# Moving the second attention's weight products and constants, regrouping the first attention's softmax by half, and storing the query squares without padding

## The chip, the cores and the metric

One Trainium2 chip, one of its cores. The metric is the device time of one execution in microseconds, taken as the median of several runs. A profile of one more execution stands beside them; all times inside the kernel come from that one.

## The reference: what is computed

A small vision tower in float32 on 16 images of 3 x 96 x 96. Its parts, in the order of the computation:

```python
h = tok(x)                                  # 36 patches of 16x16x3, layer norm, @ lin_w, layer norm, + class token and positions
h = h + attn0(layernorm(h))                 # 16 query heads of 16, one shared key and value head, rows batch x (head, token)
h = h + moe(layernorm(h))                   # 8 experts of 128, two chosen per token, and a shared one of 256
h = h + attn1(layernorm(h))                 # 16 heads of 16, attention over the HEADS' rows, three rounds
h = h + ffn(layernorm(h))                   # 256 -> 768 -> 256, weights and activations rounded to grids
```

There are 37 tokens per image, 592 in all, of width 256. The second attention is the one whose weights the change moves:

```python
for it in range(3):
    ql = qcur @ Wlq.T + blq;  kl = kcur @ Wlk.T + blk;  vl = vcur @ Wlv.T + blv     # 16 x 16, every head the same
    qs = ln(ql, lnc_w) * tscale;  ks = ln(kl, lnd_w)
    ai = softmax(qs @ ks.T / 4) @ vl
    qcur = qcur + ai;  kcur, vcur = kl, vl
```

In the kernel only the first 16 tokens of each image take part in the second attention as queries and keys (the reference slices them), so one round has 2 halves of 8 images with 256 columns each.

## The kernel before

The stages around the change, with their places:

- **Token embedding and first layer norms.** TensorE: patches x `lin_w` in three banks `y` 0, 1, 2 (L1635). VectorE: for each `y`, bias, statistics, norm, addend (L1048 to L1071); it asks ScalarE for the inverse root in between (`variance_given`, L958; `root_of_tiles`, L646). Then `layer_norm(2)` (L985) writes `xn`, tile by tile (L994). Behind `y` TensorE turns four weights (`wT` q0, o0, v1, o1) and `wkvT` (L1645), has 8 fillers, and forms the small matrices of the second attention (`wl`, `wn`, `bl`, `bq`, L1659 to L1672), which VectorE masks by head after its layer norm (L1074 to L1082). Then `turn(0)` with 10 fillers (L1696) transposes `xn`.
- **First attention.** Keys and query groups (L1710 to L1718), values (`v0`, L1719), logits of half 0 and of half 1 (`S`, L1728; 16 partitions, 37 columns each). VectorE subtracts the row maximum (`scores`, L1115), ScalarE takes exponentials (`exps`, L704), VectorE sums and inverts (`row_sums`, L1122), GpSimd multiplies (L569). VectorE interleaves halves: scores 0,0 0,1 0,2, sum 0,0, scores 0,3, then a sum of half 0 with a score of half 1 in turn. ScalarE's list alternates exponentials of half 1 with emptying of the banks below.
- **Weights of the second attention.** Behind both halves of logits TensorE computes powers of the small matrices (`pw` 0, 1), four composed weights (`wc` q, 1, 2, 3) and the constants (`cst`), L1788 to L1816. Then probabilities of half 0 are transposed (`PT`, L1750), multiplied with the values (`PV`, L1767), and so on; the projection (`wo`) follows.
- **Second layer norm.** `turn(1)` with 22 fillers (L1842), gate logits `lg` (L1846), the experts (L1866). VectorE rounds the feed-forward weights `fraw` between its expert steps (`dequantise`, L1168), after one wait for their DMAs ahead of the loop (L1253).
- **Third layer norm.** TensorE turns six banks of rounded weights (`fw`), then `turn(2)` with 6 fillers (L1882).
- **Second attention, three rounds.** Per round: logits of half 0, `query_variance` (L1925), logits of half 1, and so on. ScalarE squares the queries into `squares_n` (L812), which has the padded layout of `queries_n` (two blocks of 16 columns apart by 16), zeroed once by GpSimd (L573). TensorE then needs two products per group of 128 rows, one for each half f of the width.

DMAs that hang on these places: SyncE issues the experts' weights when `y` 2 is full (L479) and the feed-forward weights when `cst` is full (L488).

The main lines:

```python
for u in range(2):                                        # L1785
    attention_scores(u)
...
for n, name, m in (("q", "q1", q_), (1, "k1", KEY_POWER[0]), (2, "k1", KEY_POWER[1]), (3, "k1", KEY_POWER[2])):   # L1797
...
turn(1, 2, awake=22)                                      # L1842
...
ins = product(b[:, u * B + n * NH:u * B + (n + 1) * NH],  # L1932
              [(squares_n[:, u, at_ + 32 * CB * f + TF * (1 - f):...], mean_m[:, :, 0]) for f in range(KD)])
```

## Time and profile before

| what | us |
|---|---|
| median of 3 runs | 312.52 |
| lowest and highest | 310.95 and 314.73 |
| the profiled execution | 311.37 |
| its span, first to last instruction | 309.6 |
| TensorE busy | 258.7 |
| VectorE busy | 207.3 |
| ScalarE busy | 95.6 |
| GpSimd busy | 43.0 |

Times inside the kernel count from the first instruction of the span. The profiled execution is 1.77 us longer than its span, which is what lies around it. The mean granted clock of TensorE over the span is 0.956 of full speed. In the profile PE is TensorE, PEld its loading of stationary operands, DVE VectorE, ACT ScalarE, POOL GpSimd, SP SyncE. A row such as `PE bank L1608` names the engine, the tile written and the line; L1608 is the helper `product`, so the operands in the row tell which product it is.

### The profile page before, as it was taken

The page shows a single profiled execution, that of the slowest core. Times are in us where ns is not written, and L with a number is a line of the kernel's source. Part 1 is how long each engine was busy: PE and PEld are TensorE (multiplying, and loading weights), DVE is VectorE, ACT ScalarE, POOL GpSimd, SP SyncE. Part 2 cuts the span into 40 slices and gives each one's busy share as a digit, 9 for nine tenths or more (in the row PEclk, how much of TensorE's full clock was granted, in tenths as well). Part 3 has the DMA queues.
Part 4 walks back from the last instruction along what each step waited for, and adds up shares of the span by engine and source line. Part 5 has one row for each costly group of instructions (what it writes and reads, how often), then busy time and mean ns, then how long its engine had stood idle before and what let it go on. Part 6 is the DMA issues. An engine that isn't in the chain of part 4 may idle for free.

```text
span 309.6 us, 5714 instructions
## 1 busy us (share of the span) xinstructions
PE 258.7 (84%) x2276; PEld 212.8 (69%) x2276; DVE 207.3 (67%) x495; ACT 95.6 (31%) x226; POOL 43.0 (14%) x77
## 2 busy tenths in 40 slices
PE   1068999799989999999999989997769599907596
PEld 1047889698987867777776878784658376607484
DVE  0679388538705459788878946858587545999931
ACT  0045033223551251111112244744504232953000
POOL 6032001012600200000000016694000000000000
PEclk9999999995799999999999999999999899987689
DMA  7933009600062000000000000000000000000001
GB/s 180 314 62 70 2 14 300 197 4 2 2 226 83 3 0 0 0 2 0 0 2 1 0 2 0 4 2 2 1 2 0 2 0 0 0 0 3 0 34 44
DMA packets 16148, 12.10 MB, mean 39 GB/s; under 512 B 4603, under 2 KB 15578, under 8 KB 16122
## 3 DMA queue, kind: packets, MB, share of 16 engines
q1 hardware_dynamic: 13864, 10.01, 11.7%
q10 hardware_dynamic: 2258, 1.73, 1.8%
q8 instruction: 18, 0.29, 0.4%
q14 instruction: 8, 0.07, 0.1%
HBM read 11.13 MB, written 0.61 MB: 38 GB/s over the span
## 4 chain that ended last, share of the span: by engine, by line
PE 63%; DVE 18%; SPq 7%; ACT 6%; issue 4%; DMA 1%; DVEq 0%; ACTq 0%
PE bank L1608 46%; PE bank L2058 5%; SPq L465 3%; PE bank L1603 3%; PE bank L1705 3%; DVE part L1456 2%; PE bank L1767 2%; DMA cols<-in_L_attn_factor 1%; DVE big L1040 1%; ACT big L916 1%; ACT big L917 1%; DVE big L1522 1%; PE bank L1684 1%; ACT xT L686 1%; SPq L467 1%
## 5 line engine op out<-in xcount | busy, mean ns | idle before, releaser
L1608 PE MATMUL bank<-xT,big 128*128 128x296 f32 (+1 forms) x192 | 45.7, 391 | 0.0
L1608 PEld LDWEIGHTS bank<-xT,big 128*128 128x128 f32 x192 | 34.3, 190 | 9.5 <-issue 0.2
L1603 PE MATMUL bank<-ident,ones 128*128 128x128 f32 x172 | 26.0, 317 | 6.4 <-POOL queries_n L542 6.4
L1603 PEld LDWEIGHTS bank<-ident,ones 128*128 128x128 f32 x172 | 24.8, 229 | 7.3 <-POOL queries_n L542 6.4
L1608 PE MATMUL bank<-xT,fT 128*128 128x296 f32 (+12 forms) x96 | 26.2, 437 | 2.4 <-DVE xT L1477 2.4
L1608 PEld LDWEIGHTS bank<-xT,fT 128*128 128x128 f32 x96 | 18.1, 201 | 9.5 <-issue 2.7
L1608 PE MATMUL bank<-big,cur 128*128 128x256 f32 (+1 forms) x100 | 23.3, 381 | 0.7 <-DVE cur L1230 0.7
L779 ACT ACTIVATE cen<-bank 128x296 f32<-128x296 f32 x20 | 8.3, 417 | 46.4 <-PE bank L1608 40.7
L1608 PEld LDWEIGHTS bank<-big,cur 128*128 128x128 f32 (+1 forms) x100 | 18.0, 182 | 4.9 <-DVE cur L1230 1.5
L1243 DVE SCALAR_TENSOR_TENSOR h<-bank,route,h 128x256 f32<-128x256 f32 (+1 forms) x40 | 17.0, 477 | 2.9 <-PE bank L1608 2.9
L1456 DVE TENSOR_REDUCE part<-big 128x1 f32<-128x296 f32 (+2 forms) x18 | 13.1, 732 | 8.1 <-ACT big L909 8.0
L588 POOL TENSOR_SCALAR big<-keys_n,k_w 128x256 f32<-128x256 f32 x24 | 15.9, 683 | 4.6 <-DVE keys_n L1335 4.6
L2058 PE MATMUL bank<-fT,big 128*128 128x256 f32 (+1 forms) x60 | 15.4, 424 | 0.5 <-DVE big L1453 0.5
L1608 PE MATMUL bank<-big 128*128 128x256 f32 (+1 forms) x60 | 13.2, 380 | 1.9 <-DVE big L1040 1.9
L2058 PEld LDWEIGHTS bank<-fT,big 128*128 128x128 f32 (+1 forms) x60 | 12.4, 208 | 3.4 <-DVE big L1453 0.8
L1608 PEld LDWEIGHTS bank<-big 128*128 128x128 f32 (+1 forms) x60 | 10.8, 182 | 4.0 <-issue 2.1
L1608 PE MATMUL bank<-probs,rsd 37*128 37x257 f32 (+1 forms) x10 | 4.6, 648 | 10.1 <-DVE first L977 10.1
L1011 DVE BATCH_NORM_STATS2 st<-big 96x6 f32<-96x256 f32 x18 | 6.1, 408 | 10.1 <-DMA big<-in_x 10.1
L1230 DVE TENSOR_TENSOR cur<-cen,bank 128x296 f32<-128x296 f32 x20 | 9.0, 460 | 4.8 <-PE bank L1608 4.4
L580 POOL COPY cur<-xT 128x256 f32<-128x256 f32 x2 | 0.8, 408 | 77.5 <-ACT xT L688 77.5
L2026 PE MATMUL bank<-ident,mx 128*128 128x128 f32 x4 | 1.3, 333 | 11.8 <-DVE mx L1459 10.0
L1608 PEld LDWEIGHTS bank<-probs,rsd 37*128 37x128 f32 (+1 forms) x10 | 3.0, 312 | 11.2 <-DVE first L977 10.4
(294 smaller groups left out, 496.7 us busy)
## 6 DMA issues: line engine op xcount, KB each, us to landing
big<-in_x SPq DMA_DIRECT2D x3, 576.0 KB, 10.6
big<-in_L_ffn_w_gate SPq DMA_DIRECT2D x2, 512.0 KB, 5.4
big<-in_L_ffn_w_up SPq DMA_DIRECT2D x2, 512.0 KB, 6.5
big<-in_L_ffn_w_down SPq DMA_DIRECT2D x1, 1024.0 KB, 8.7
big<-in_L_tok_lin_w SPq DMA_DIRECT2D x3, 256.0 KB, 9.9
small<-in_L_ffn_w_gate SPq DMA_DIRECT2D x1, 768.0 KB, 4.6
small<-in_L_ffn_w_up SPq DMA_DIRECT2D x1, 768.0 KB, 6.5
small<-in_L_ffn_w_down SPq DMA_DIRECT2D x1, 768.0 KB, 9.2
```

The costliest lines, as they stand in the source:

```text
L465: sp.dma_start(col[:, 2 * c:2 * c + 2], v[c], allow_slow_non_contiguous=True).then_inc(cols_in, 16)
L588: ins = pool.tensor_scalar(fkeys[a - 1][:, u, :, n, :], keys, k_w[:, a - 1, n:n + 1], 1.0, ALU.mult, ALU.mult)
L779: empty(act.activation(silu[:, c, :], b[:, 0:HP], ACT.Silu))
L1011: ins = dve.bn_stats(st[0:96, 3 * w + c, :], pv[:, c, :, w, :])
L1230: empty(dve.tensor_tensor(hid[:, e % 3, c * HP:(c + 1) * HP], silu[:, c, :], b[:, 0:HP], ALU.mult))
L1243: ins = dve.scalar_tensor_tensor(out=v, in0=src, scalar=route[0:n, t, e:e + 1], in1=v, op0=ALU.mult, op1=ALU.add)
L1456: return dve.tensor_reduce(part[:, n:n + 1], v, AX.X, ALU.max, apply_absolute_value=True)
L1603: pe.matmul(b[:, 0:P], ones[:, :], ident[:, :], start=True, stop=True)
L1608: ins = pe.matmul(out_, a_, b_, start=(n == 0), stop=(n == len(pairs) - 1))
L1705: ins = pe.matmul(b[32 * j:32 * j + m, at_:at_ + 4 * T].rearrange("p (u c) -> p u c", u=2), w(k), xq[:, k, :, 2 * j * T:2 * (j + 1) * T], ...
L1767: ins = pe.matmul(b[32 * q:32 * q + 32, m * 2 * T:(m + 1) * 2 * T].rearrange("p (i t) -> p i t", i=2), vals[0:G3, 3 * u + g, s, h_, :], by ...
L2058: ins = pe.matmul(b[0:rows, 0:D], gate[:, o * NT + t * P:o * NT + t * P + rows], fT[2][:, o, :], start=(o == 0), stop=(o == FC - 1))
```

## The change

1. TensorE and VectorE form and mask the small matrices (`wl`, `wn`, `bl`, `bq`) between `y` 1 and `y` 2; VectorE does so while it waits for the root of `y` 1.
2. `pw` 0, `pw` 1, `wc` q and `wc` 1 move ahead of `turn(0)`; the transposes of v1 and o1, `wc` 2 and `wc` 3 move between the first attention's projection and `turn(1)`; the constants `cst` move between `fw` and `turn(2)`. ScalarE's emptying moves with them. Fillers go from 8 to 0 (`wl`), 10 to 2, 22 to 0 and 6 to 0.
3. The values' product and its handling by VectorE and GpSimd stand between the two halves of the logits; VectorE and ScalarE do all of half 0, then all of half 1.
4. The squares of the queries are stored densely, in order image, f, token; one product per group of 128 rows. GpSimd's zeroing and ScalarE's wait for it go.
5. The feed-forward weights' DMAs wait for `wc` 3; VectorE waits for them at its first reduction. The experts' weights still wait for `y` 2, which comes later. The query bias constant is computed early, with its own semaphore.

The diff, cut to its core:

```diff
 def fills():
-    for i in range(3):
+    for i in range(2):
         f.append((("y", i), "dve"))
-    for n in ("q0", "o0", "v1", "o1"):
-        f.append((("wT", n), "act"))
-    f.append((("wkvT",), "act"))
     f.append((("wl",), "dve"))
     f.append((("wn",), "dve"))
     f.append((("bl",), "dve"))
     f.append((("bq",), "act"))
+    f.append((("y", 2), "dve"))
+    f.extend((("wT", n), "act") for n in ("q0", "o0"))
+    f.append((("wkvT",), "act"))
+    f.extend((("pw", n), "act") for n in range(2))
+    f.extend((("wc", n), "act") for n in ("q", 1))
...
-    f.append((("v0",), "dve"))
     for u in range(2):
         f.extend((("S", u, j), "dve") for j in range(4))
-    f.extend((("pw", n), "act") for n in range(2))
-    f.extend((("wc", n), "act") for n in ("q", 1, 2, 3))
-    f.append((("cst",), "act"))
+        if not u:
+            f.append((("v0",), "dve"))
...
+    f.extend((("wT", n), "act") for n in ("v1", "o1"))
+    f.extend((("wc", n), "act") for n in (2, 3))
...
     f.extend((("fw", n), "dve" if n % 2 else "act") for n in range(6))
+    f.append((("cst",), "act"))
...
-            filled(sp, ("cst",))
+            filled(sp, ("wc", 3))
...
             for u in range(2):
+                if u:
+                    values_by_slot()
                 for j in range(4):
                     pool.wait_ge(sums_ready, 4 * u + j + 1)
...
-            pool.memset(squares_n[:, :, :], 0.0).then_inc(squares_cleared, 1)
...
             for j in range(2):
                 root_of_tiles(j)
+            b = take(act, ("bq",))
+            empty(act.copy(bqh[:, :], b[:, 0:2 * NH]))
+            attn_weight("q0")
+            attn_weight("o0")
             b = take(act, ("wkvT",))
             empty(act.copy(wkvT.rearrange("p k n d -> p (k n d)"), b[:, 0:4 * HD]))
             root_of_tiles(2)
+            for n in range(2):
+                powers(n)
...
             inverse_root(P, slice(0, TT))
+            for n in ("q", 1):
+                composed_weights(n)
             turned(0)
...
             for j in range(4):
                 exps(0, j)
-            powers(0)
-            exps(1, 0)
...
+            for j in range(4):
+                exps(1, j)
             for t in range(RT):
                 probs_turned(0, t)
...
+            attn_weight("v1")
+            attn_weight("o1")
+            composed_weights(2)
             inverse_root(P, slice(0, TT))
+            composed_weights(3)
             turned(1)
...
+            constants()
             turned(2, c_lna, (0, 2))
...
-                act.activation(padded(squares_n, u), padded(queries_n, u), ACT.Square).then_inc(q_squared, 1)
+                act.activation(squares_n[:, u, :].rearrange("p (b f t) -> p f b t", b=CB, f=KD),
+                               queries_n[:, u, TF:].rearrange("p (f b t) -> p f b t", f=KD, t=2 * TF)[:, :, :, 0:TF],
+                               ACT.Square).then_inc(q_squared, 1)
...
-                variance_given(ins)
+                variance_given(ins, small_matrices if j == 1 else None)
...
-            scores(0, 0)
-            scores(0, 1)
-            scores(0, 2)
-            row_sums(0, 0)
-            scores(0, 3)
...
+            for j in range(4):
+                scores(0, j)
+            values()
+            for j in range(4):
+                row_sums(0, j)
+            for j in range(4):
                 scores(1, j)
-            row_sums(1, 0)
-            scores(1, 3)
-            for j in range(1, 4):
+            for j in range(4):
                 row_sums(1, j)
...
                 if step == 0:
+                    dve.wait_ge(ffn_in, 48)
...
             for j in range(3):
                 b = fill(("y", j))
...
+                if j == 1:
+                    pe.wait_ge(attn_w_in, 16 * N_ATTN_W)
+                    small_matrices()
...
+            attn_weight("q0")
+            attn_weight("o0")
...
+            emptied(pe, ("bl",))
+            for n in range(2):
+                if n:
+                    emptied(pe, ("pw", 0))
+                b = fill(("pw", n))
...
+            composed_weights("q", "q1", q_)
+            composed_weights(1, "k1", KEY_POWER[0])
...
-            turn(0, 1, awake=10)
+            turn(0, 1, awake=2)
...
-            for u in range(2):
-                attention_scores(u)
...
+            attention_scores(0)
+            values_of_tokens()
+            attention_scores(1)
...
-            turn(1, 2, awake=22)
+            attn_weight("v1")
+            attn_weight("o1")
+            composed_weights(2, "k1", KEY_POWER[1])
+            emptied(pe, ("pw", 1))
+            composed_weights(3, "k1", KEY_POWER[2])
+            turn(1, 2)
...
-            turn(2, 3, awake=6)
+            pe.wait_ge(q_bias_ready, 1)
...
+            turn(2, 3)
...
                     for n in range(2):
-                        at_ = 32 * 4 * n
                         ins = product(b[:, u * B + n * NH:u * B + (n + 1) * NH],
-                                      [(squares_n[:, u, at_ + 32 * CB * f + TF * (1 - f):at_ + 32 * CB * f + TF * (1 - f) + P],
-                                        mean_m[:, :, 0]) for f in range(KD)])
+                                      [(squares_n[:, u, n * P:(n + 1) * P], mean_m[:, :, 0])])
```

## Rows read from the trace of the kernel before

**Rows 1.** The page: busy time by engine, and granted clock in 40 slices.
```profile
PE 258.7 (84%) x2276; PEld 212.8 (69%) x2276; DVE 207.3 (67%) x495; ACT 95.6 (31%) x226; POOL 43.0 (14%) x77
...
PEclk9999999995799999999999999999999899987689
```
**Rows 2.** Windows: length, busy time of each engine (instructions), then granted clock, DMA share, GB/s.
```profile
70.90:81.00 10.10, 9.53 (x88) 9.16 (x87) 9.71 (x24) 5.09 (x10) 3.29 (x5) 0.50 0.00 0
...
248.00:249.00 1.00, 1.00 (x5) 0.73 (x4) 0.22 (x1) 0.41 (x1) 0.00 (x0) 0.86 0.00 0
```
**Rows 3.** The chain that ended last, in order of time: start, length, what.
```profile
44.55 1.75 PE bank L1649 x16
...
67.95 2.40 PE bank L1736 x80
...
76.20 10.05 PE bank L1608 x68
...
87.00 1.78 ACT cur L712 x5
...
89.02 2.27 PE bank L1767 x123
...
100.73 4.91 PE bank L1603 x44
...
244.40 15.65 PE bank L1608 x52
```
**Rows 4.** TensorE's timeline: start, busy, line, instruction, count, idle before.
```profile
77.64 5.35 PE L1608 MATMUL bank<-wlT,small 128*128 128x128 f32 x32
...
175.90 1.50 PE L1603 MATMUL bank<-ident,ones 128*128 128x128 f32 x12
177.77 1.79 PE L1684 MATMUL bank<-ident,xn 128*128 128x128 f32 x10 [0.36 <-DVE xn L994]
...
189.97 1.95 PE L1608 MATMUL bank<-mean_m,qT 128*128 128x8 f32 x16
```
**Rows 5.** GpSimd's timeline: softmax factors, and keys spread over heads.
```profile
82.61 2.34 POOL L569 TENSOR_TENSOR big<-big,row_sum 128x370 f32<-128x370 f32 x3 [0.86 <-DVE row_sum L1126]
...
185.73 4.89 POOL L588 TENSOR_SCALAR big<-keys_n,k_w 128x256 f32<-128x256 f32 x4 [4.59 <-DVE keys_n L1335]
...
199.98 6.08 POOL L588 TENSOR_SCALAR big<-keys_n,k_w 128x256 f32<-128x256 f32 x10
```
**Rows 6.** VectorE's timeline: layer norms, small matrices, softmax of the first attention.
```profile
43.76 0.25 DVE L1060 BATCH_NORM_AGGREGATE mv<-st 128x2 f32<-128x6 f32 x2
44.61 0.16 DVE L1064 TENSOR_TENSOR masked<-rstd,passes 128x2 f32<-128x2 f32 x1 [0.60 <-ACT rstd L644]
...
47.70 0.40 DVE L1053 TENSOR_TENSOR h<-bank,sqr 80x256 f32<-80x256 f32 x1
...
54.05 0.68 DVE L1075 TENSOR_TENSOR wlT<-bank,head_of 128x512 f32<-128x512 f32 x1
...
54.91 0.16 DVE L1085 TENSOR_SCALAR temps<-temps 128x3 f32<-128x3 f32 x1
...
70.33 0.54 DVE L1118 TENSOR_REDUCE row_max<-bank 128x10 f32<-128x370 f32 x1 [1.63 <-PE bank L1736]
...
71.37 0.53 DVE L1118 TENSOR_REDUCE row_max<-bank 128x10 f32<-128x370 f32 x1
...
82.45 0.48 DVE L1125 TENSOR_REDUCE row_sum<-big 128x10 f32<-128x370 f32 x1
...
83.10 0.48 DVE L1125 TENSOR_REDUCE row_sum<-big 128x10 f32<-128x370 f32 x1
...
103.32 1.70 DVE L994 TENSOR_SCALAR xn<-h,mv,rstd 128x256 f32<-128x256 f32 x5 [0.68 <-ACT rstd L644]
```
**Rows 7.** ScalarE's timeline: last query group, and the copies of turned tiles.
```profile
65.79 0.52 ACT L700 ACTIVATE qT<-bank,bqh 128x148 f32<-128x148 f32 x1 [0.94 <-PE bank L1705]
...
106.11 1.54 ACT L686 COPY xT<-bank 128x256 f32<-128x256 f32 x6 [2.90 <-PE bank L1684]
```

More of the change, by code:

```diff
@@ L673, in _ @@
             root_of_tiles(2)
-            b = take(act, ("bq",))
-            empty(act.copy(bqh[:, :], b[:, 0:2 * NH]))
+            for n in range(2):
+                powers(n)
             def turned(n, scales=None, js=range(3)):
@@ L718, in heads_out @@
                                b[:, 0:8 * T].rearrange("p (b i t) -> p b i t", b=4, i=2)))
-            def powers(n):
-                b = take(act, ("pw", n))
-                empty(act.copy(wlT[:, 5 + 3 * n:8 + 3 * n, :].rearrange("p m n -> p (m n)"), b[:, 0:3 * P]))
-            def composed_weights(n):
-                b = take(act, ("wc", n))
-                empty(act.mul(composed[n].rearrange("p k o -> p (k o)"), b[:, :], KSCALE))
             def constants():
@@ L1633, in _, with small_matrices @@
                     full(ins)
+            def small_matrices():
+                ci = rep_i.rearrange("p h d -> p (h d)")
+                cc_ = rep_c.rearrange("p h d -> p (h d)")
+                mats = ((0, cc_), (1, cc_), (2, ci))
+                w8 = [wl8[:, n, :, :].rearrange("p h d -> p (h d)") for n in range(3)]
+                b = fill(("wl",))
+                pe.wait_ge(wl8_ready, 1)
+                for m, (n, c_) in enumerate(mats):
+                    product(b[:, m * P:(m + 1) * P], [(w8[n], c_)])
+                full(product(b[:, 3 * P:4 * P], [(ci, w8[1])]))
+                b = fill(("wn",))
+                full(product(b[:, 0:P], [(ci, w8[2])]))
+                b = fill(("bl",))
+                for m, (n, c_) in enumerate((*mats, (1, ci))):
+                    ins = product(b[:, m:m + 1], [(c_, blr[:, n:n + 1])])
+                full(ins)
+                b = fill(("bq",))
+                full(product(b[:, 0:2 * NH], [(bq8.rearrange("p n d -> p (n d)"), ident[0:2 * NH, 0:2 * NH])]))
             pe.wait_ge(patch_w_in, 16 * NC)
@@ L1642, in _, with attn_weight @@
                 full(ins)
[L1644 to L1645 removed]
+                if j == 1:
+                    pe.wait_ge(attn_w_in, 16 * N_ATTN_W)
+                    small_matrices()
+            def attn_weight(n):
                 b = fill(("wT", n))
@@ L1718, in _, with values_of_tokens @@
                 full(ins)
-            b = fill(("v0",))
-            for u in range(2):
-                for g in range(3):
-                    rows = (3 if g < 2 else 2) * T
-                    at_ = CH * u + G3 * g
-                    ins = product(b[0:rows, (3 * u + g) * HD:(3 * u + g + 1) * HD],
-                                  [(xT[:, k, at_:at_ + rows], wkvT[:, k, 1, :]) for k in range(KD)])
-            full(ins)
+            def values_of_tokens():
+                b = fill(("v0",))
+                for u in range(2):
+                    for g in range(3):
+                        rows = (3 if g < 2 else 2) * T
+                        at_ = CH * u + G3 * g
+                        ins = product(b[0:rows, (3 * u + g) * HD:(3 * u + g + 1) * HD],
+                                      [(xT[:, k, at_:at_ + rows], wkvT[:, k, 1, :]) for k in range(KD)])
+                full(ins)
             def attention_scores(u):
```

158 lines of the change are left out of this document (63 added, 95 removed).

## The prediction

> **What bounds the kernel now.** I read the page's totals and the row of granted clock first, then the chain that ended last in order of time, then each engine's timeline around the moved work. The totals [rows 1] show TensorE busy 84% of the span: what is taken out of its queue counts where TensorE ends the wait, and only there. The clock row shows the one deep dip of the first two thirds, in slices 10 and 11 of 40 (about 70 to 85 us). 
>
> The chain [rows 3] then reads: logits of half 0 (67.95), VectorE's softmax steps, the weight products and constants until 86.25, ScalarE's five copies of turned probabilities (87.00), attention times values (89.02), fillers until 105.64. The softmax was not the end of that wait: GpSimd had finished half 0 much earlier and all of half 1 at 82.61+2.34 = 84.95 [rows 5]. Taking the products out makes VectorE's softmax the bound between logits and values.
>
> **Part 1: first layer norm.** TensorE now does 20 small instructions between `y` 1 and `y` 2, 20 x 0.11 = 2.2 us [rows 3]. VectorE takes `y` 2 only at 47.70, without waiting; its bank was full at 44.55 [rows 3] and would now be at about 46.9, so that is covered; the cost if the cover went is at most 2.2. VectorE's three small operations took 0.86 us (54.05 to 54.91). They now start at 43.76+0.25 = 44.01 and end at 44.9, where the next step began at 44.61: +0.3 us on the chain [rows 6]. TensorE must then fit q0, o0, kv, `pw` 0, `pw` 1, `wc` q and `wc` 1 behind `y` 2: 8+2+12+16 = 38 instructions, 4.4 us, plus an estimated 1.3 us waiting for ScalarE to empty `pw` 0, behind its root for `y` 2. That ends near 52.6; two fillers end at 53.1, when the first normalised tiles are ready. Fillers (8 and 8 products) went, so the place was there. The new waits on `bl` and on the query bias (set by VectorE ahead of the patches) are met when TensorE comes to them. Taken: +0.3, ends 0 and +1.5 (root queued behind copies). The expert weight DMAs, released by `y` 2, go 2.5 us later, needed only near 110: nothing.
>
> **Part 2: logits to values.** The values product leaves the front of half 0, so logits start when the last query group is in, 65.79+0.52 = 66.31 on ScalarE [rows 7], say 66.4. They need 2.4 [rows 3]: 68.8. VectorE then runs, by its own periods [rows 6]:
> - four logits steps at 1.04 (70.33 to 71.37): 68.8+4.15 = 72.95;
> - the values' four small operations, 0.7, a little under the 0.86 of the three above: 73.65. Their bank is filled by then (2.2 us of TensorE behind half 0);
> - four row sums at 0.65 (82.45 to 83.10): 76.25. GpSimd multiplies at 0.78 each (2.34/3 [rows 5]), done about 77.6; its multiplication of the values by slot, now behind these four, ends near 78.9 and is needed at 83;
> - four logits steps of half 1: 80.4. Half 1 of the logits is filled by 75, even at half clock.
>
> ScalarE's copies of half 0 stand in its queue behind the last exponential of half 1, at 80.9. Five copies take 1.9 (87.00 to 89.02 with the start), so values start at 83.0, with Part 1's 0.3 at 83.3, against 89.02: **-5.7 us**. Turning half 0 may run at half clock (15 transposes, 3.7 us from 77.8, done 81.6) and still be ahead of the last copies. Half 1 is ready at 84.5, before the values of half 0 are through. Ends: -4.5 (a wait missed on ScalarE) and -6.5.
>
> **Part 3: the clock after it.** This is the price. The dense products are gone from between logits and values; in their place TensorE has narrow work, then idles. I expect the clock to fall near 71 as now, and nothing to bring it back before the values start. From rows: it came back at 81.0, 4.8 us after the dense stretch began at 76.20; and at about 248.3 (0.86 of full clock in that microsecond), 3.9 us after work restarted at 244.40 [rows 2, 3]. So some 4.6 us from 83.3 run at half clock, half of them lost: **+2.3 us**. Ends: 0 (turning half 0 brings it back) and the whole stretch to the output projection, 100.73-89.02 = 11.7 us doubled.
>
> **Part 4: second layer norm.** Behind the projection TensorE has four sets (v1, o1, wc 2, wc 3): 8+16 instructions, 2.7 us, instead of 44 fillers, 4.91 us, which ended at 105.64, though VectorE's tiles were written from 103.32 on. ScalarE copies v1, o1 and wc 2 before the root, which it started at 102.67 (103.32 less VectorE's idle 0.68). `wc` 2 is filled at 100.7+16x0.11 = 102.5, its copy ends at 103.2, so the root is 0.5 late, tiles from 103.8. Transposes follow the tiles, the second pair of copies ends at 106.05 instead of 106.11+1.03 = 107.14 [rows 6, 7]: **-1.1 us**. Ends: -1.5, and +2 if the clock falls where fillers were. The second feed-forward weights' three DMAs now wait for `wc` 3 (they stood behind the constants at 86.3) and land during the first experts. VectorE's wait for them moves into the loop before the first reduction, at expert 1: covered; a late landing would cost only that reduction's place.
>
> **Part 5: layer norm before the second attention.** The constants take 3.3 us (from 77.64+5.35 = 82.99 to 86.25 [rows 3, 4]) and replace 12 fillers, which end at 177.40. They start at 175.95 and end at 179.2, so the transposes that started at 177.77 start 1.4 late. Before, they followed VectorE (10 in 1.79); now all tiles are there and they run at 0.12: 0.5 back. ScalarE's five constants (0.75, from 86.25 to 87.00) run beside the first of them. **+1.1 us**, ends +0.5 and +1.8. VectorE behind this wait has the middle copy only.
>
> **Part 6: squares of queries.** Each of three rounds has 16 instructions in 1.95 us between the logits of its two halves, at 0.12 each although only 8 columns stream [rows 4]; now 8, 0.97 us. Is TensorE last there? GpSimd's spread of the keys that half 1 needs ends at 185.73+4.89 = 190.6 and 199.98+6.08 = 206.1 [rows 5]; half 1 could start at 190.9 and 206.7: just cleared. VectorE waited for both. The clearing of the padding on GpSimd had nobody waiting for it. **-2.9 us** for three, ends -1.5 (rounds caught by the spread) and -3.1. The Trainium skill (TensorE: Matmul & The Clock Gate, Back-to-back issue gap) lets a matmul of 1 to 64 columns take about 25 ns. By that, 24 instructions fewer would give an estimated 0.6 us, not 2.9; the rows' 122 ns decides here, since every one of these products has a stationary operand of 128 columns of its own.
>
> **Sum.** -5.7+2.3-1.1+1.1-2.9 = -6.3 us. The profiled execution took 311.37 us, 1.77 around its span of 309.6; by it 305.1. The runs' median is 312.52, 1.15 higher, and less 6.3 gives 306.2. I say 306.0.
>
> **The rivals.**
> - *The clock stays down* (slower). If narrow logits, transposes and 74-column products do not bring it back, the stretch from values to projection is doubled: 11.7 instead of 2.3, and v1, o1, wc 2 hold the root 2 us more: -6.3+9.4+2 = +5.1, 317.6. For it: the clock fell under a fully busy TensorE. Against: it stayed full through the values at 89 to 98. It decides from 8.6 us lost, 17 us at half clock. 5%.
> - *The clock comes back early*, by turning half 0: -2.3 more, 303.8. For it: work from 77.8. Against: TensorE idles before and behind it. 14%.
> - *The second layer norm loses*: without fillers the clock falls before the router or ScalarE's root is later: +2.5, 308.5. For it: less work on TensorE. Against: the gaps are about 1 us. 14%.
> - *The removed squares were nearly free*: a narrow product may cost what the values' products do, 2.27/123 = 18 ns [rows 3]; then 24 fewer give -0.4 instead of -2.9: 308.5. Against: 0.12 in all three rounds. 4%. The Trainium skill's figure above points the same way.
> - *The softmax is not shortened*: a queue order missed, values start no earlier than 87: 310. 8%.
>
> **How the numbers follow.** The forecast has 55%. The range 302.0 to 311.0 leaves out 1 in 10 at each end: the low end is early clock and the good ends of Parts 2 and 4, the high end a late softmax or a clock down for twice as long. About 1% can be told from no change, 3.1 us: faster means below 309.4. All but the first and last rivals lie below it, so faster 0.79, same 0.15, slower 0.06.
>
> **What would show it.** Values of half 0 start near 83; half clock from about 71 to 88 instead of 81; ScalarE's last exponential of half 1 directly ahead of its copies; no fillers near 101 and the first transposes at the tiles' pace; constants ahead of late transposes in the third layer norm; three stretches of 8 instructions in 1 us. It is wrong if values start after 86, if half clock lasts past 95, or if half 1's logits in the second attention wait for GpSimd.

## The result, and the profile after

The changed kernel took 311.94 us (median of 20 executions, 308.33 to 316.34) beside 314.06 for the kernel before (20 on the same chip): ratio 0.9926 [0.9896, 0.9955], some 2.3 us faster. On a second chip it was 0.9934 [0.9899, 0.9968]. The forecast was 6.5 us faster, 306.0, with a range to 311.0; the median lies outside it.

Two profiled executions of the same changed kernel stand beside the one of before, because their granted clocks differ and with them the place where the time went. The profile of before is one of its quicker executions (311.37 us, at the highest clock that it reached), so the differences below set the changed kernel against before at its best. Their totals:

| profiled execution | span | mean granted clock | TensorE busy |
|---|---|---|---|
| before | 309.6 | 0.956 | [rows 1] |
| after, first | 311.1 | 0.917 | 255.3 |
| after, second | 306.9 | 0.933 | 250.1 |

The time follows the clock within one kernel: of the 20 executions, the five at 0.933 took 308.3 to 309.0 us, the four at 0.928 took 309.8 to 310.6, the eight at 0.917 or 0.918 took 312.5 to 313.9, the two at 0.908 took 316.1 and 316.3. Every ratio in this document leaves out the executions that took over 1.5% longer than the same kernel's fastest.

The page, first execution after, then second (busy time by engine, granted clock in 40 slices; as [rows 1]):

```profile
span 311.1 us, 5489 instructions
...
PE 255.3 (82%) x2164; PEld 208.2 (67%) x2164; DVE 207.6 (67%) x495; ACT 95.4 (31%) x226; POOL 43.5 (14%) x76
...
PEclk9999989996559999999999959999999899977689
```

```profile
span 306.9 us, 5489 instructions
...
PE 250.1 (82%) x2164; PEld 203.7 (66%) x2164; DVE 207.4 (68%) x495; ACT 95.2 (31%) x226; POOL 43.5 (14%) x76
...
PEclk9999999996579999999999979999999599977689
```

TensorE's timeline of the first execution, from the small matrices to the second half of the first attention (to be held against [rows 3] at 44.55, 67.95 and 89.02):

```profile
44.14 0.37 PE L1621 MATMUL bank<-ident,bq 16*128 16x16 f32 x2
44.44 4.50 PE L1621 MATMUL bank<-big 128*80 128x256 f32 x12
...
57.12 0.71 PE L1746 MATMUL bank<-xT,wkvT 128*32 128x148 f32 x16 [0.73 <-ACT xT L705]
...
63.73 4.24 PE L1746 MATMUL bank<-xT,wT_q 128*32 128x148 f32 x127 [1.79 <-issue]
69.24 2.44 PE L1779 MATMUL bank<-kT,qT 16*128 16x37 f32 x80 [1.27 <-ACT qT L721]
71.60 3.96 PE L1621 MATMUL bank<-wkvT,xT 128*111 128x16 f32 x24
75.49 4.50 PE L1779 MATMUL bank<-kT,qT 16*128 16x37 f32 x80
80.76 3.51 PE L1793 MATMUL bank<-ident,big 128*111 128x128 f32 x15 [0.77 <-POOL big L577]
86.78 4.18 PE L1810 MATMUL bank<-cur,small 111*32 111x74 f32 x128 [2.51 <-ACT cur L733]
```

The same view of the second execution:

```profile
44.59 2.82 PE L1621 MATMUL bank<-big 128*80 128x256 f32 x12
...
68.19 2.44 PE L1779 MATMUL bank<-kT,qT 16*128 16x37 f32 x80 [1.25 <-ACT qT L721]
...
73.75 4.50 PE L1779 MATMUL bank<-kT,qT 16*128 16x37 f32 x80
...
85.03 3.97 PE L1810 MATMUL bank<-cur,small 111*32 111x74 f32 x128 [1.81 <-ACT cur L733]
```

`y` 2 (12 instructions) takes 2.82 us in the second and 4.50 in the first. The logits of half 1 take 4.50 in both, against 2.44 for the same 80 instructions of half 0. The values start at 86.78 or 85.03 instead of 89.02.

VectorE in the first execution (to be held against [rows 6] at 47.70, 70.33 and 71.37): it now waits for `y` 2, and for the logits of half 1. In the second it waits for neither.

```profile
48.98 0.42 DVE L1076 TENSOR_TENSOR h<-bank,sqr 80x256 f32<-80x256 f32 x1 [0.83 <-PE bank L1621]
...
79.03 0.22 DVE L1140 RECIPROCAL row_sum<-row_sum 128x10 f32<-128x10 f32 x1
80.01 0.54 DVE L1132 TENSOR_REDUCE row_max<-bank 128x10 f32<-128x370 f32 x1 [0.76 <-PE bank L1779]
```

The windows show where the clock was at its lower level: nearly all of 71 to 93 us in the first execution and of 71 to 89 in the second; most of 44 to 48 and of 177 to 188 in the first, where the kernel before has full clock. A clock of 0.5 is the lower level for the whole window, 1.00 the upper one. Columns as in [rows 2]; first execution:

```profile
71.00:93.00 22.00, 18.72 (x285) 18.04 (x281) 14.19 (x37) 7.32 (x17) 7.48 (x10) 0.53 0.01 1
44.00:48.00 4.00, 4.00 (x14) 2.63 (x14) 3.86 (x12) 0.56 (x3) 0.00 (x0) 0.57 0.00 0
...
177.00:188.00 11.00, 10.08 (x48) 9.59 (x49) 2.33 (x7) 3.14 (x11) 0.76 (x2) 0.53 0.01 1
```

Second execution:

```profile
44.00:48.00 4.00, 4.00 (x25) 3.17 (x26) 3.83 (x13) 0.67 (x4) 0.00 (x0) 1.00 0.00 0
71.00:89.00 18.00, 14.72 (x246) 14.18 (x245) 13.35 (x36) 6.29 (x14) 7.48 (x10) 0.53 0.01 2
...
238.00:246.00 8.00, 5.62 (x13) 3.86 (x14) 3.37 (x11) 2.04 (x4) 0.00 (x0) 0.57 0.01 2
```

The layer norm before the second attention, first execution (to be held against [rows 4] at 175.90, 177.77 and 189.97):

```profile
174.93 0.51 PE L1621 MATMUL bank<-cols,wlT 128*128 128x2 f32 x4
...
178.24 0.57 PE L1621 MATMUL bank<-cols,wlT 128*128 128x2 f32 x2
178.66 2.38 PE L1725 MATMUL bank<-ident,xn 128*128 128x128 f32 x10
181.96 3.75 PE L1621 MATMUL bank<-xT,wT_k 128*128 128x128 f32 x16 [0.92 <-ACT xT L707]
...
193.23 1.12 PE L1621 MATMUL bank<-big,queries_n 128*32 128x128 f32 x32
194.28 1.06 PE L1621 MATMUL bank<-mean_m,qT 128*128 128x8 f32 x8
```

And where it stands in the second:

```profile
175.53 1.29 PE L1725 MATMUL bank<-ident,xn 128*128 128x128 f32 x10
177.94 3.41 PE L1621 MATMUL bank<-xT,wT_k 128*128 128x128 f32 x16 [1.11 <-ACT xT L707]
...
187.75 1.12 PE L1621 MATMUL bank<-big,queries_n 128*32 128x128 f32 x32
```

Put together from the starts of TensorE's groups (differences to before of each stretch; each column sums to the difference of the spans):

| stretch | before | after, first | after, second | forecast |
|---|---|---|---|---|
| to the logits of half 0 | 67.88 | +1.4 | +0.3 | -1.2 |
| logits to values | 21.14 | -3.6 | -4.3 | -4.5 |
| values to experts | 21.64 | +1.2 | +0.3 | +1.2 |
| experts to third transposes | 67.11 | +1.9 | +1.4 | +1.4 |
| transposes to key projections | 2.70 | +0.6 | -0.3 | -0.3 |
| key projections to logits of second attention | 8.46 | +2.8 | +1.3 | 0 |
| these logits to the second attention's projection | 42.07 | -2.5 | -2.5 | -2.9 |
| from there to the end | 78.6 | -0.3 | +1.0 | 0 |
| sum | 309.6 | +1.5 | -2.7 | -6.3 |

### The profile page after: what moved, and what is told of

It is laid out like the page before. It is cut to its first block, busy times and chain, and to the rows that moved or that the text cites. A ratio compares the mean times of both kernels' runs of the same rounds, so it can differ in the third digit from the quotient of the medians.

```text
span 311.1 us, 5489 instructions
## 1 busy us (share of the span) xinstructions
PE 255.3 (82%) x2164; PEld 208.2 (67%) x2164; DVE 207.6 (67%) x495; ACT 95.4 (31%) x226; POOL 43.5 (14%) x76
## 4 chain that ended last, share of the span: by engine, by line
PE 65%; DVE 16%; ACT 8%; DMA 5%; issue 4%; ACTq 0%; DVEq 0%
PE bank L1621 48%; DMA sqr<-in_L_tok_ln_b 5%; PE bank L2087 5%; PE bank L1746 3%; PE bank L1779 2%; PE bank L1810 2%; DVE part L1469 2%; ACT big L668 1%; PE bank L1725 1%; PE bank L1616 1%; ACT big L926 1%; ACT big L927 1%; PE bank L1854 1%; DVE big L1535 1%; ACT xT L705 1%
## 5 line engine op out<-in xcount | busy, mean ns | idle before, releaser
L1616 PE MATMUL bank<-ident,ones 128*128 128x128 f32 x84 | 15.2, 354 | 6.4 <-POOL queries_n L545 6.4
L1616 PEld LDWEIGHTS bank<-ident,ones 128*128 128x128 f32 x84 | 14.5, 266 | 7.1 <-POOL queries_n L545 6.4
L595 POOL TENSOR_SCALAR big<-keys_n,k_w 128x256 f32<-128x256 f32 x24 | 17.5, 749 | 7.4 <-DVE keys_n L1348 7.4
L1621 PE MATMUL bank<-big 128*128 128x256 f32 (+1 forms) x60 | 15.1, 415 | 1.6 <-ACT big L668 1.6
L1621 PEld LDWEIGHTS bank<-big 128*128 128x128 f32 (+1 forms) x60 | 11.6, 196 | 4.5 <-issue 3.1
```

Source lines behind the costliest of these rows:

```text
L595: ins = pool.tensor_scalar(fkeys[a - 1][:, u, :, n, :], keys, k_w[:, a - 1, n:n + 1], 1.0, ALU.mult, ALU.mult)
L1616: pe.matmul(b[:, 0:P], ones[:, :], ident[:, :], start=True, stop=True)
L1621: ins = pe.matmul(out_, a_, b_, start=(n == 0), stop=(n == len(pairs) - 1))
```

## The experiments

All ratios are to the kernel before on the same chip. In most of these kernels single executions spread over 5 us or more, so that differences under 0.004 of the ratio decide nothing. A theory and a rival in an expectation are the two outcomes that the run was to tell apart.

### One part alone

**Squares alone** (the kernel before with the squares dense):

```diff
-  [(squares_n[:, u, at_ + 32*CB*f + TF*(1-f):... + P], mean_m[:, :, 0]) for f in range(KD)]
+  [(squares_n[:, u, n * P:(n + 1) * P], mean_m[:, :, 0])]
```

> The kernel before with one part of the change, the query squares stored densely (one product per group of 128 rows, no clearing). My theory: TensorE is last in each of the three rounds and 24 of 48 instructions of 0.12 us go, so 2.9 us less than the kernel before (ratio 0.991), and the three stretches take 0.97 us each. Rival, the squares are covered by GpSimd's spread of keys: under 1 us less, and the second half's logits wait for GpSimd.

Measured 0.989 [0.9835, 0.9946]. TensorE's timeline:

```profile
197.24 1.06 PE L1607 MATMUL bank<-mean_m,qT 128*128 128x8 f32 x8
198.23 1.01 PE L1607 MATMUL bank<-big,queries_n 128*32 128x128 f32 x28
```

Half as many instructions take about half the time, and the next group follows at once. Repeated:

> The kernel before with the squares made dense, a second time, beside the run without them. Theory (squares give -2.9 to -3.5 us and the rest of the change nothing): ratio 0.987 to 0.993, at or below the changed kernel's. Rival (the squares are worth little, the first reading was luck): 0.995 to 1.0.

Measured 0.9968 [0.9925, 1.0011], at the high edge between the two expectations. Its best execution (308.6 at a clock of 0.955) lies 2.5 us under the best of before on that chip (311.1 at 0.956). The clock moves this reading as well: in the profile of the repeat (clock 0.934) the stretch with the squares is 2.7 us shorter than before, but the experts start at 114.71 instead of 110.66, with half clock in parts of 48 to 56 (0.79) and of 86 to 96 (0.66), where the profile of before has full clock, although TensorE's work up to there is unchanged.

**All but the squares** (after, squares padded again):

```diff
-  [(squares_n[:, u, n * P:(n + 1) * P], mean_m[:, :, 0])]
+  [(squares_n[:, u, at_ + 32*CB*f + TF*(1-f):... + P], mean_m[:, :, 0]) for f in range(KD)]
```

> The changed kernel with the squares of the queries padded again, so that only the moved weight products, the order by half and the constants are left of the change. Theory (the moves give nothing net, the squares give all): ratio to the kernel before 0.998 to 1.006, and each of the three query variances takes 1.95 us in 16 instructions again, at full clock. Rival (the moves are worth a part of their own, forecast -3.4 us): ratio 0.986 to 0.994.

Measured 1.0008 [0.9977, 1.0039]. TensorE's timeline has the old form back:

```profile
192.53 1.95 PE L1622 MATMUL bank<-mean_m,qT 128*128 128x8 f32 x16
```

So the moved weight products, the order by half and the moved constants together gave nothing that can be measured; the rival, a gain of their own, is out. Best executions: 311.5 at a clock of 0.928, beside 311.1 at 0.956 before: the same time at a lower clock. After itself, on the same chip:

> The changed kernel itself, on the same chip as the two runs with one part of it each. Both theories: ratio about 0.9926, as measured. Were the parts to add (squares -3.3 us and the moves x), it gives the moves' x a second time: theory 0 to +2 us, so 0.989 to 0.996; rival -3 us, so 0.978 to 0.984.

Measured 0.9934 [0.9899, 0.9968]. Moves (0.9977 to 1.0039) and squares (0.9925 to 1.0011) add to it within their intervals.

**Order of the first attention alone** (kernel before; half by half with the values' product between, weight products where they were):

```diff
-    f.append((("v0",), "dve"))
     for u in range(2):
         f.extend((("S", u, j), "dve") for j in range(4))
+        if not u:
+            f.append((("v0",), "dve"))
```

> The kernel before with only the order of the first attention changed: values' product and handling between the two halves of the logits, VectorE by half; weight products stay between logits and values. Theory (the clock and the weight products decide, not VectorE's order): nothing gained, between 0.5 less and 2.5 us more than the kernel before, since TensorE's products fill the wait either way and the second half's logits come after a values' product at half clock. Rival (the order itself saves time): 2 us less or more.

Measured 1.0095 [1.0059, 1.0131], 3 us slower. TensorE's timeline:

```profile
71.80 4.50 PE L1743 MATMUL bank<-kT,qT 16*128 16x37 f32 x80
76.23 1.65 PE L1613 MATMUL bank<-wlT 128*128 128x128 f32 x6
...
79.89 5.72 PE L1613 MATMUL bank<-wlT,small 128*128 128x128 f32 x32
...
91.64 1.57 PE L1774 MATMUL bank<-cur,small 111*32 111x74 f32 x85 [1.06 <-ACT cur L718]
```

With the products in place the values start at 91.64, 2.6 us later than before: half 1 of the logits now runs at half clock throughout (4.50 us for its 80 instructions, where both halves together took 6.17), and the weight products behind it start at 76.23 instead of 73.98.

**The order put back** (after, with the values' product ahead and the softmax interleaved as in before; the weights stay moved):

```diff
-            attention_scores(0)
-            values_of_tokens()
-            attention_scores(1)
+            for u in range(2):
+                attention_scores(u)
```

> The changed kernel with only the order of the first attention put back (values' product ahead of both halves of the logits, VectorE and GpSimd interleaved as before); the weight products stay moved. Theory: once the products are gone, the order matters little: the values' product costs 1 us ahead of the logits, the second half's logits no longer come late (0.8 us) and the last exponential comes 0.9 us sooner; within 1 us of the changed kernel (ratio to before 0.990 to 0.996). Rival (grouping by half is what pays): 2 us or more slower than the changed kernel.

Measured 0.9885 [0.9825, 0.9945], and the values start at 87.72. The order by half brings the start of the values 0.9 us forward in the profile (86.78 with it, at the same clock of 0.917), and no gain in the total that can be measured.

### The clock

**Small matrices behind `y` 2** instead of ahead of it:

```diff
-                if j == 1:
+                if j == 2:
                     pe.wait_ge(attn_w_in, 16 * N_ATTN_W)
                     small_matrices()
```

> The changed kernel with the small matrices (16 rows) behind the third product of patches instead of ahead of it, VectorE masking them in the root wait of that one. Clock theory: the third product of patches is no longer at half clock (2.6 instead of 4.5 us), VectorE does not wait for it, and the first transposes start 1 us sooner; 0.5 to 1.5 us less than the changed kernel, more in the runs in which the clock had fallen there. Rival (the late start comes from ScalarE's longer queue): no change.

Measured 0.9965 [0.9924, 1.0006]: not better than after. `y` 2 kept full clock, but the half clock moved along with the narrow products and now lay on the dense ones behind them; windows:

```profile
47.00:58.00 11.00, 9.85 (x47) 9.09 (x48) 8.26 (x33) 4.40 (x12) 1.40 (x2) 0.53 1.15 321
```

**Fillers beside the softmax** (after, fillers ahead of turning half 0, and between that and the values; TensorE's waits for the probabilities and for the values move behind them, so that the fillers run in the wait):

```diff
                     b = fill(("PT", u, t))
+                    if t == 0 and u == 0: keep_awake(b, 2)   # 4 instructions in the trace
...
                     b = fill(("PV", u, x))
+                    if x == 0 and u == 0: keep_awake(b, 5)   # 10
```

> The changed kernel with 2 fillers ahead of the first turned probabilities and 5 between them and the values of half 0, where TensorE idles 0.8 and 2.5 us. Clock theory: the clock is back at full before or early in the values' products, which then take 2.3 instead of 4.2 us; 1.5 to 2.5 us less than the changed kernel (ratio to the kernel before about 0.986), mean granted clock up by 0.01. Rival (the values are late for another reason): no change in time, whatever the clock.

> The changed kernel with the first attention's 7 fillers once more, as the one to compare with beside the next three. If the first reading holds, 0.981 to 0.989 of the kernel before; if it was luck of the runs, 0.990 to 0.995, where the changed kernel stands.

Measured 0.9846 [0.9807, 0.9884], then on another chip 0.9921 [0.9882, 0.9961], which lies where the second expectation put it if the first reading was luck. TensorE's timeline of the repeat:

```profile
84.21 2.05 PE L1616 MATMUL bank<-ident,ones 128*128 128x128 f32 x10
86.75 2.28 PE L1816 MATMUL bank<-cur,small 111*32 111x74 f32 x128 [0.49 <-ACT cur L733]
```

The values run at full clock, 2.28 instead of 4.18 us, and the experts start at 107.02 in an execution with `y` 2 at half clock, where after has 109.66. The fillers bring the clock back where they stand. Over the whole kernel a gain beyond after's 0.993 is not shown by these two readings. In the profile of the first one the experts started 1.75 us earlier than in after's second execution (105.25 beside 107.00), and by the logits of the second attention it was 1.0 later (188.79 beside 187.75): the transposes and key projections ahead of these took 2.38 and 3.75 us there, instead of 1.29 and 3.41.

**Constants among the experts** (after, in three pieces behind experts 2, 4 and 6):

```diff
                     down(min(e - 1, NE))
+                if e in (2, 4, 6):
+                    constant_products((2, 4, 6).index(e))
```

> The changed kernel with the constants' products (2 columns each) in three pieces behind experts 2, 4 and 6 instead of one stretch ahead of the third transposes, where no filler stands now. Clock theory: no half clock near 178 to 188; 2.6 us from the place and about 2.5 us from the clock saved, 3.3 us of TensorE paid back in the experts; net 1 to 3 us less than the changed kernel (ratio to before about 0.986), mean clock up by 0.015. Rival (only the place costs, the clock falls there anyway): the same time as the changed kernel and half clock at the key projections still.

Measured 0.9896 [0.9851, 0.9941]. Windows:

```profile
177.00:188.00 11.00, 8.29 (x65) 7.28 (x64) 6.46 (x18) 5.43 (x15) 1.44 (x3) 1.00 0.01 1
```

Full clock there, and key projections of 2.06 us instead of 3.75. But from the start of the experts to the third transposes it now takes 70.56 us, 1.6 more than in the first execution of after. From the start of the experts to the second attention's logits it is 81.6 us, against 83.6 in after's first execution, 80.8 in its second and 78.3 before: whether a net gain is left depends on which of them it is held against. Of the two combinations below with the same three pieces, one has 8.45 us from the key projections to these logits, as here and before (8.46), the other 11.2. Over all profiles: in the seven profiles without constants at this place the key projections took 2.05 or 2.06 us in five and 3.54 and 3.75 in two (the first run of the squares alone, and the values last); in all eleven profiles with them, or with four of them, 3.37 to 3.76. Without the constants the clock mostly stays up there, not always; with them it fell each time.

**Combinations.** Fillers and constants in three pieces; that, with the values' product behind both halves; fillers, and six more among the constants; fillers, and three more among the small matrices; fillers, with four constant products left in place and eleven behind experts 3 and 6, which was run twice. In the third and the fourth of these, the expectation sets out from the fillers alone. Edits beside those above:

```diff
...
-            attention_scores(0); values_of_tokens(); attention_scores(1)   # values last
+            attention_scores(0); attention_scores(1); values_of_tokens()
...
             product(b[:, 2:4], [...])                                      # third norm, six times
+            pe.matmul(b[:, 2 * P:3 * P], ones[:, :], ident[:, :], start=True, stop=True)
...
             b = fill(("wn",))                                              # first norm: two here, one at bl
+            for _ in range(2): pe.matmul(b[:, 2 * P:3 * P], ones[:, :], ident[:, :], start=True, stop=True)
...
+            constant_products(0)                                           # split: cst 11..14 stay
             turn(2, 3)
...
+                if e in (3, 6): constant_products(1 + (3, 6).index(e))     # split: cst 0..5, 6..9
```

> The changed kernel with both the fillers in the first attention and the constants in three pieces behind experts 2, 4 and 6. If the two losses are separate stretches of half clock, the gains add: 0.9846 x 0.9896 / 0.9926 = 0.982 to the kernel before, and a mean clock near 0.95. Rival (the runs share one loss): no better than the fillers alone, 0.985.

> The same, and the values' product behind both halves of the logits, so that the second half's logits are not behind 3.7 us of values at half clock. Theory (VectorE's 0.8 us wait for the second half and 0.6 us of the values' steps go): 0.8 to 1.4 us less than without it, ratio about 0.978. Rival (the turned probabilities then wait for the values' product): the same or slower.

> The same, and 6 fillers (12 instructions, 1.4 us) between the constants' products, which are 30 instructions with 2 streamed columns. Clock theory: the narrow stretch is what lowers the clock there; with dense products in it the clock stays, the 2.8 us that the key and query projections lost come back and 1.4 us of fillers are paid on the path: 1 to 1.5 us less than with the first attention's fillers alone, clock up by 0.01. Rival (the constants themselves lower it, whatever stands between): 1.4 us more, half clock from about 174 on as before.

> The first attention's fillers, and 3 more (0.7 us) between the small matrices of 16 rows ahead of the third product of patches. Clock theory: half clock in that product (4.5 instead of 2.6 us, in most profiles) comes less often: 0 to 1.5 us less. Rival (the stretch is narrow all the same): 0 to 0.7 us more, since VectorE then gets its bank later.

> The first attention's fillers, and the constants split: the four products needed at the start of the second attention (8 instructions, 1 us) stay ahead of the third transposes, the other eleven (22 instructions, 2.4 us) go behind experts 3 and 6. Theory: TensorE is no longer late at the transposes (-1 us) and the narrow stretch is short enough for the clock to stay (-2.8), 2.4 paid in the experts: 1 to 1.5 us less than with the fillers alone, transposes at the tiles' pace. Rival (as with the spread: nothing left over): within 0.5 us of it.

> The changed kernel with fillers beside the first attention's softmax and eleven of the fifteen constant products behind two of the experts, a second time. Theory (half clock costs the gain: 17 us of it less than in the changed kernel): ratio 0.984 to 0.990, lower than the changed kernel's in this call by 0.004 or more. Rival (what is taken out of one stretch comes back in another): within 0.003 of the changed kernel's.

| kernel | ratio | span, clock of the profile | values start | experts start | logits of second attention |
|---|---|---|---|---|---|
| fillers, three pieces | 0.9898 [0.9840, 0.9955] | 307.9, 0.933 | 87.06 | 107.31 | 188.95 |
| same, values last | 0.9900 [0.9865, 0.9935] | 308.7, 0.939 | 85.52 | 106.49 | 190.91 |
| fillers, third norm | 0.9891 [0.9826, 0.9957] | 307.4, 0.938 | 84.39 | 104.64 | 189.55 |
| fillers, first norm | 0.9948 [0.9914, 0.9982] | 309.9, 0.928 | 89.74 | 110.02 | 190.73 |
| fillers, split | none (6 executions) | 306.6, 0.944 | 85.16 | 105.40 | 187.52 |
| fillers, split, again | 0.9933 [0.9894, 0.9971] | 308.3, 0.939 | 86.59 | 106.85 | 189.06 |
| after, again | 0.9934 [0.9899, 0.9968] | 306.9, 0.933 | 85.03 | 107.00 | 187.75 |

No theory of these six is borne out by its ratio. Fillers and three pieces were to add up to 0.982, the values last to give 0.978; both stayed at 0.99. The 0.9891 of the third norm is within the noise of the fillers alone (0.9921). Six fillers between the constants, one each, did not hold the clock; in that profile the key projections read

```profile
178.31 3.75 PE L1621 MATMUL bank<-xT,wT_k 128*128 128x128 f32 x16 [0.92 <-ACT xT L707]
```

as in the first execution of after, which is what that run's rival expected. The split version starts the experts 1.6 us earlier than after's second execution, in its own first profile, and is back at it by the second attention (187.52 beside 187.75). On the same chip it came out at 0.9933 beside 0.9934: the rival expected that, what is taken out of one stretch comes back in another. Three fillers among the small matrices did not help: `y` 2 still took 4.47 us at half clock. It started 2.8 us later than in after's first execution, of which 1.4 stood already ahead of the first small matrix. The lowest time of any execution is the split version's, 305.7, but on the chip that had it beside after, the ratios were the same. A version that surely beats after was not found.

## Why the prediction was wrong

The direction was right, the size was 2.8 times too large. The step that failed is the price of the clock: the sum charged half clock in one place, behind the logits (Part 3), and put it at nothing behind the small matrices (Part 1) and behind the constants (Part 5). The second, smaller one is the start of the logits. By its own steps, each against the two profiled executions of after:

- **Part 6, the squares (-2.9): right.** 8 instructions in 1.06 instead of 16 in 1.95, three times; the stretch is 2.53 us shorter in both executions. GpSimd's spread of the keys did not catch the rounds. The rival that the squares are nearly free is out in the profile: eight columns behind a stationary operand of 128 columns cost about 0.12 us per instruction here. The Trainium skill (TensorE: Matmul & The Clock Gate, Back-to-back issue gap) has about 25 ns for 1 to 64 columns, and in the same section it says that in a stream of weight loads and matmuls both together set the spacing. The trace agrees with the second and not with the first, which was the wrong figure to take for these products. The two whole readings (0.989, 0.9968) hold the profile's 0.8% between them.
- **Part 1 (+0.3): mis-sized where the clock fell.** The small matrices, 16 rows deep, keep TensorE busy without a gap, and the granted clock is at its lower level in most of 44 to 48 (0.57 of full) in one execution, at full in the other. Over the 13 profiles that have them ahead of `y` 2, it took 4.47 to 4.50 us in eight and 2.82 in five. In the first, `y` 2 ends 1.7 late (4.50 instead of 2.82) and VectorE waits 0.83 for it. The prediction had said that this cover holds ("its bank would be full at about 46.9"); it did not allow for `y` 2 itself at half clock. The key projection starts at 57.12, +1.7 instead of +0.3; at 55.95, +0.5, in the execution where the clock stayed.
- **Part 2's start of the logits (66.4, with Part 1 66.7): wrong by 1.5.** In the second execution they start at 68.19. Two pieces of time that the profile calls "issue" (the engine waits for nothing that it shows) explain 1.4 of it. The first stands between the query groups; the kernel before has 1.13 us there, which the prediction took over with the times of before:

```profile
61.04 4.72 PE L1705 MATMUL bank<-xT,wT_q 128*32 128x148 f32 x138 [1.13 <-issue]
```

  After has 1.79 and 1.94. The second is the 0.68 us between ScalarE's last query group and the first logits (67.52 to 68.19 in the chain below), for which the prediction had put 0.09. What makes this time was not tried. The profiles narrow it down: the first gap is 1.13 and 1.40 with the weight products where they were, 1.79 to 2.03 in thirteen profiles with them moved, the order put back among these (1.89), and absent in the three profiles that had half clock at 53 us. So the order by half did not cause it.
- **Part 2's softmax on VectorE: right until half 1.** Four logits steps, the values' four operations and four row sums went as written, 71.66 to 79.25, that is 7.6 us against the forecast 7.45 (68.8 to 76.25). Then "half 1 of the logits is filled by 75, even at half clock" failed: values' product 3.96 and half 1 4.50 us at half clock fill its first bank at 80.0, and VectorE waits 0.76. In the second execution the chain of waits goes through TensorE's two groups until 78.29, but VectorE itself was through with its row sums at 78.21, so there this wait cost less than 0.1:

```profile
67.00 0.52 ACT qT L721
67.52 0.68 issue
68.19 2.44 PE bank L1779 x80
70.63 3.19 PE bank L1621 x24
73.82 4.47 PE bank L1779 x80
78.29 0.54 DVE row_max L1132
...
83.02 1.78 ACT cur L733 x5
...
85.03 3.97 PE bank L1810 x128
```

  From there on the forecast holds to 0.1: four steps, the last exponential, five copies, values. They start 1.7 later than forecast in this execution, 3.5 later in the first. The sign of being wrong, values after 86, came in the first execution (86.78), close to what the rival of the unshortened softmax (8%) had said, but for a reason that it didn't name: no queue order was missed.
- **Part 3 (+2.3): right.** The clock fell at 71 and was back at 89 in the second execution and at 93 in the first, forecast 88. From the values' start to the end of the projection the first lost 2.34 us and the second 1.43, forecast 2.3.
- **Part 4 (-1.1): right.** No fillers, four sets of products; from the projection's end (100.83) to the experts (109.66) 8.8 us, against 9.9 before.
- **Part 5 (+1.1): mis-sized, and its consequence missed.** From the start of the experts to the logits of the second attention the first execution lost 5.3 us and the second 2.5; this is the largest missing term in the first, and about as large as the start of the logits in the second. The sum took the constants as 3.3 us of work and nothing more. The key projections of the kernel before:

```profile
180.47 2.05 PE L1608 MATMUL bank<-xT,wT_k 128*128 128x128 f32 x16 [0.91 <-ACT xT L688]
```

  In the first execution the clock falls behind the constants (0.53 of full in 177 to 188): the transposes take 2.38 instead of the second execution's 1.29, the key projections 3.75 instead of 2.05, and from these to the logits of the second attention 2.8 us are lost. In the second execution it is 1.3. With the constants among the experts the stretch was at full clock in two kernels of three, and it was at half clock in all eleven profiles that had constants ahead of it. So the constants are a cause that the runs support, and not the only one.
- **The clock in the last stretch** took another 1.0 in the second execution (0.57 of full in 238 to 246). No cause is known for it.

In the second execution the forecast missed by 3.6 us: 1.5 at the start of the logits, 1.4 around the constants, 1.0 in the last stretch and 0.4 at the squares came on top, 0.2 at the softmax; between values and experts it did 0.9 better than forecast.

Summed over Parts 1 to 5, the forecast had -3.4 us. The profiles give -0.2 (second execution: -2.7, less -2.5 for the squares) and +4.0 (first), and the run with all but the squares gives 1.0008. What the softmax's shorter path saved, 3.6 to 4.3 us, was spent again: at half clock in `y` 2, in the values and around the key projections, on the constants' own place on the path (1.4 to 1.9 us), and on the later start of the logits. That the spread of the executions goes with the clock is shown within one kernel by the times at each clock; why one execution drops at 44 us and another doesn't stays open. That the lost clock is what kept the total down is read from these stretches and not proved by a run: fillers or moved constants restored the clock in single stretches, and no version with them is shown to be faster than after.

## What to carry to other kernels

Dense products that look like ballast in a wait can be what holds TensorE's clock for the work behind them: before moving them, sum up the stretches of narrow products (few rows or few columns) that are left without them, and cost every dense group behind such a stretch at half clock as one of the cases. Work put into a wait was free here only where the clock stayed: behind the constants, 2 columns wide and 3.7 us long, the first execution lost about as much again at half clock, the second 1.3. And a change whose effect is an interplay with the clock is measured by many executions: each part alone, beside the whole, on one chip.

## What was not expected of the hardware

- The granted clock at the same instructions differs from execution to execution: `y` 2 took 2.82 or 4.50 us. After has mean clocks of 0.933, 0.928, 0.922, 0.917 and 0.908 with medians of about 308.6, 310.6, 311.4, 313.4 and 316.2 us; before's at its highest clock, 0.956, took 311.1 to 311.9 on the last chip.
- A fully busy TensorE lost its clock behind products of 16 rows (busy 4.00 of 4.00 us in 44 to 48, clock 0.57) and of 2 columns (10.08 of 11.00 in 177 to 188, clock 0.53), as it does on the logits in [rows 2]. Being busy was not enough.
- Three fillers of full size among the small matrices did not help (`y` 2 still 4.47 us), nor did six between the constants (key projections still 3.75); ten recorded instructions directly ahead of the values did, with four ahead of the turning (values 2.28 instead of 4.18).
